# Strassen products whose partial sums add up in PSUM, in a graph-attention layer with a residual and a layer norm

## What is computed

```python
output = einsum('bni,io->bno', x, weight)
q = einsum('bni,io->bno', x, wq)
k = einsum('bni,io->bno', x, wk)
alpha = einsum('bno,bmo->bnm', q, k)
alpha = maximum(alpha, 0.0) * (adj != 0)
alpha = softmax(alpha, axis=1)
y = x + einsum('bnm,bmo->bno', alpha, output)
out = layernorm(y, axis=-1)
```

## Time and profile before

| | |
|---|---|
| Median of 3 timed runs | 557.91 us |
| The profiled execution's own time | 558.32 us |
| Its span, first to last instruction | 556.4 us |
| Mean granted TensorE clock over the span | 0.988 of full |

### The profile page before, as it was taken

How to read it: one execution, slowest core, us unless ns; L and a number is a source line. 1 busy time by engine, 2 the same in 40 slices (tenths; PEclk the granted TensorE clock), 3 DMA queues, 4 the chain that set the end, 5 groups by cost and what they waited for, 6 DMA issues and landing times.

```text
span 556.4 us, 10947 instructions
## 1 busy us (share of the span) xinstructions
PE 530.2 (95%) x3852; PEld 498.4 (90%) x3852; DVE 455.6 (82%) x842; ACT 288.6 (52%) x635; POOL 315.1 (57%) x220
## 2 busy tenths in 40 slices
PE   5886899999999999999999999999999999999994
PEld 4776899899998989999898989989898998989993
DVE  5797769879696988969697896969789796978776
ACT  4744446374553726465373646546364654646263
POOL 2699906639193664919375582928558292844002
PEclk9997999999999999999999999999999999999998
DMA  8206325231432523142152414224150423403021
GB/s 285 93 0 228 114 77 190 75 122 69 140 127 77 188 75 140 48 163 101 75 188 75 158 37 179 79 91 173 75 181 25 171 75 110 154 0 152 0 78 76
DMA packets 23636, 62.12 MB, mean 112 GB/s; under 512 B 1216, under 2 KB 1216, under 8 KB 21696
## 3 DMA queue, kind: packets, MB, share of 16 engines
q1 hardware_dynamic: 23616, 61.87, 30.8%
HBM read 45.09 MB, written 16.78 MB: 111 GB/s over the span
## 4 chain that ended last, share of the span: by engine, by line
PE 67%; DVE 16%; issue 10%; ACT 2%; DMA 2%; SPq 1%; DVEq 1%; POOLq 0%; POOL 0%; ACTq 0%
PE ring L216 13%; PE ring L218 13%; PE ring L217 13%; DVE sums L561 6%; PE s_bank L216 6%; PE s_bank L218 6%; PE s_bank L217 6%; PE o_bank L216 5%; PE o_bank L217 3%; PE o_bank L218 3%; DVE t_lo L547 3%; DMA sums<-in_wk_t 2%; DVE xn L606 2%; ACT t_hi L407 2%; DVE g_lo L547 1%
## 5 line engine op out<-in xcount | busy, mean ns | idle before, releaser
L781 POOL TENSOR_TENSOR s_lo<-xs,s_hi 128x512 fp32r<-128x512 f32 x64 | 92.3, 1455 | 78.8 <-ACT s_hi L396 72.9
L561 DVE TENSOR_TENSOR sums<-sums,ring 128x512 f32<-128x512 f32 x155 | 100.5, 682 | 8.2 <-PE ring L218 7.2
L775 POOL TENSOR_TENSOR a_lo<-xt,a_hi 128x512 fp32r<-128x512 f32 x60 | 94.6, 1605 | 0.0
L432 ACT ACTIVATE squares<-xn,neg_mean 128x512 f32<-128x512 f32 x64 | 46.3, 724 | 86.7 <-DVE neg_mean L613 81.0
L786 POOL TENSOR_TENSOR rstd<-var_eps,minus_half 128x4 f32<-128x4 f32 x15 | 15.3, 1018 | 129.8 <-DVE var_eps L617 129.8
L407 ACT CAST t_hi<-sums 128x512 fp32r<-128x512 f32 x64 | 39.7, 621 | 73.9 <-DVE sums L561 73.1
L216 PE MATMUL s_bank<-t_hi,a_hi 128*128 128x256 f32 x256 | 73.2, 286 | 2.4 <-DVE t_lo L547 2.4
L547 DVE TENSOR_TENSOR v_lo<-sums,v_hi 128x512 fp32r<-128x512 f32 x60 | 72.7, 1228 | 2.3 <-ACT v_hi L412 0.2
L216 PE MATMUL ring<-s_hi,g_hi 128*128 128x256 f32 x256 | 72.7, 284 | 1.4 <-DVE g_lo L547 1.4
L218 PE MATMUL s_bank<-t_hi,a_lo 128*128 128x256 f32 x256 | 73.2, 286 | 0.0
L217 PE MATMUL s_bank<-t_lo,a_hi 128*128 128x256 f32 x256 | 73.1, 286 | 0.0
(11 more groups left out here) (102 smaller groups left out, 1636.0 us busy)
## 6 DMA issues: line engine op xcount, KB each, us to landing
xn<-in_x SPq DMA_DIRECT2D x16, 1024.0 KB, 5.2
xt<-in_x_t SPq DMA_DIRECT2D x15, 1024.0 KB, 4.8
out<-xn SPq DMA_DIRECT2D x15, 1024.0 KB, 4.2
adj<-in_adj_t SPq DMA_DIRECT2D x16, 512.0 KB, 3.3
xt<-in_x_t SPq DMA_DIRECT2D x4, 256.0 KB, 5.2
xn<-in_w SPq DMA_DIRECT2D x4, 256.0 KB, 5.3
xn<-in_wq_t SPq DMA_DIRECT2D x1, 1024.0 KB, 8.7
sums<-in_wk_t SPq DMA_DIRECT2D x1, 1024.0 KB, 10.7
```

The costliest lines, as they stand in the source:

```text
L432: nc.scalar.activation(squares[:], xn[:, slot, r], ACT.Square, bias=neg_mean[:, r:r + 1], accum_out=square_sum[:, r:r + 1]).then_inc(squar ...
L561: nc.vector.tensor_tensor(summed(c), whole, ring[(at + product) % 4][:], op).then_inc(combined, 1)
L775: nc.gpsimd.tensor_tensor(a_lo[:, slot, a], xt[:, a], a_hi[:, slot, a].bitcast(F32), ALU.subtract).then_inc(a_lo_ready, 1)
L781: nc.gpsimd.tensor_tensor(s_lo[:, s], xs[:, s], s_hi[:, s].bitcast(F32), ALU.subtract).then_inc(s_lo_ready, 1)
```

## The change

In T and V the products are now made in 14 half products, each one 128-row half of the result (six matmuls), in a new order: P2,0; P1,0; P1,1; P7,0; P6,0; P6,1; P7,1; P5,0; P5,1; P2,1; P3,0; P3,1; P4,0; P4,1. P1, P6, P5 and P3 accumulate in one place: `chain`, two banks of which T has one half of the columns (`chain_t`) and V the other (`chain_v`). P7 and then P4 accumulate in `bank_y`, and P2 fills `bank_z`. ScalarE copies the chain away after P1 (to c1), after P6 (to c2) and after P5 (to c3), each by halves, six copies, and TensorE waits for the copy of a half before it adds the next product to it. What stands in the chain after P3 is block C12 itself (called A12 as a block of T or V), and is split straight from PSUM. VectorE makes three sums: C22 = c3 + bank_y before P4 is added, C11 = c1 + bank_z, C21 = c2 + bank_y at the end; for the last, the fourth right operand has its sign turned (D4 for T4). They are called A22, A11 and A21 in the splits. T's P1 of the next pair waits until V's part of the chain is split (`v_lo_ready` at `4 * p - 1`). The scaled softmax weights of a pair (`split_p`) move on ScalarE and on VectorE from the V stage of its step into the T stage of the next one, and for pair 15 behind all steps. ScalarE makes a_hi of the next pair behind t_hi of A12, where it was at the head of T.

T of pair 0 is a plain product like V of pair 0: 48 matmuls of 512 columns. It comes ahead of the last quarter of V of pair 0 (now in an `o_bank`). ScalarE writes g_hi straight from PSUM; the G sums T1 to D4 and their splits are only needed by pair 1 but stand on VectorE ahead of the splits of T of pair 0. The sums of x's blocks for pair 0 (GpSimd), with their splits, are gone.

```diff
+        chain = ctx.enter_context(nc.psum_tensor("chain", [P, 2, 2, N], F32))
+        bank_y, bank_z = bank("bank_y"), bank("bank_z")
+        chain_t, chain_v = chain[:, :, 0], chain[:, :, 1]
+        ring = [chain[:, 0], chain[:, 1], bank_y[:], bank_z[:]]
         s_bank = [bank(f"s_bank{i}") for i in range(2)]
         o_bank = [bank(f"o_bank{i}") for i in range(2)]
...
-            def wait_for_bank(i, m):
...
+            def fill_t(p, slot, first=False):
+                m = t_matrix(p)
+                if first:
+                    pe.wait_ge(gt_lo_ready, 4)
                 else:
-                    before = {P1: -PRODUCTS + C22, P6: -PRODUCTS + C12, P5: -PRODUCTS + C11,
-                              P7: -PRODUCTS + C21, P2: U2, P4: U4}[i]
-                    pe.wait_ge(combined, PRODUCTS * m + before + 1)
...
+                    sum_taken(m - 1, 2)
+                x_split(p, 3)
+                t_half(P2, 0, slot, bank_z)
+                if not first:
+                    pe.wait_ge(v_lo_ready, 4 * p - 1)
+                t_half(P1, 0, slot, chain_t)
+                t_half(P1, 1, slot, chain_t)
+                if not first:
+                    sum_taken(m - 1, 3)
+                xs_split(p, 1)
+                t_half(P7, 0, slot, bank_y)
+                copy_taken(m, 1)
+                xs_split(p, 2)
+                t_half(P6, 0, slot, chain_t)
+                copy_taken(m, 2)
+                t_half(P6, 1, slot, chain_t)
+                t_half(P7, 1, slot, bank_y)
...
+                t_half(P3, 0, slot, chain_t)
+                copy_taken(m, 6)
+                t_half(P3, 1, slot, chain_t)
+                sum_taken(m, 1)
+                x_split(p, 4)
+                t_half(P4, 0, slot, bank_y)
+                t_half(P4, 1, slot, bank_y)
...
+            def fill_first_t():
+                for k in range(K):
+                    pe.wait_ge(g_lo_ready, (2, 4, 5, 6)[k])
+                    h, kk = k // 2, k % 2
+                    for j in range(K):
+                        if k == 0 and j < R - 1:
+                            pe.wait_ge(v_lo_ready, j + 1)
+                        last = add_chunk(ring[j], g_parts(k, j), (a_hi[:, 0, h::2, kk], a_lo[:, 0, h::2, kk]),
+                                         k == 0, k == K - 1)
+                        if k == K - 1:
+                            last.then_inc(t0_filled, 1)
...
+            def step(p, slot, first=False):
+                fill_t(p, slot, first)
                 fill_o(p - 1, first)
                 fill_s(p, slot)
-                fill_v(p, slot, at + PRODUCTS, first)
+                fill_v(p, slot, first)
             fill_first_v()
             fill_g()
+            fill_first_t()
             fill_last_of_first_v()
-            fill_first_t()
             fill_s(0, 0, first=True)
-            step(1, 1, PRODUCTS, first=True)
-            step(2, 0, 3 * PRODUCTS)
+            step(1, 1, first=True)
+            step(2, 0)
...
+            def copy_part(m, i, c, src, dst, reader, first=False):
+                if not first:
+                    act.wait_ge(summed, SUMS * (m - 1) + reader)
+                act.wait_ge(filled, HALVES * m + DONE[i, c])
+                nc.scalar.copy(dst[:, c], src[:, c]).then_inc(copied, 1)
+            def copy_p1(m, src, first=False):
+                copy_part(m, P1, 0, src, c1, 2, first)
+                copy_part(m, P1, 1, src, c1, 2, first)
...
+            def split_v(p, u):
+                m = v_matrix(p)
+                if u == A12:
+                    act.wait_ge(filled, HALVES * m + DONE[P3, 1])
+                    whole = chain_v
+                else:
+                    act.wait_ge(summed, SUMS * m + {A22: 1, A11: 2, A21: 3}[u])
+                    whole = {A22: c22, A11: c11, A21: c21}[u]
+                g, j = u // 2, u % 2
+                nc.scalar.copy(v_hi[:, M * g:M * g + M, j], whole).then_inc(v_hi_ready, 1)
...
+            def step(p, slot, more=True, first=False):
+                m = t_matrix(p)
+                copy_p1(m, chain_t, first)
+                split_p(p - 1, 0)
+                copy_p6(m, chain_t, first)
+                split_p(p - 1, 1)
+                copy_p5(m, chain_t, first)
+                split_p(p - 1, 2)
+                act.wait_ge(s_filled, 2 * p)
+                split_t(p, A22)
+                split_p(p - 1, 3)
+                split_t(p, A11)
+                split_t(p, A12)
                 if more:
-                    for k in range(4):
-                        if first and k == 0:
-                            act.wait_ge(v0_filled, R)
-                            act.wait_ge(xt_loaded, 16 * p + 16)
-                            nc.scalar.copy(a_hi[:, 0, A11], xt[:, A11]).then_inc(a_hi_ready, 1)
-                        else:
-                            split_a(p + 1, 1 - slot, k)
-                act.wait_ge(s_filled, 2 * p)
-                for c in SPLITS:
-                    split_t(p, t_matrix(p), c)
+                    split_a(p + 1, 1 - slot, 0)
+                split_t(p, A21)
+                if more:
+                    for k in range(1, 4):
+                        split_a(p + 1, 1 - slot, k)
                 for r in range(R):
                     centred_squares(p - 1, 1 - slot, r)
                 exponent(p, 0)
                 exponent(p, 1)
-                copy_first(v_matrix(p), at + PRODUCTS)
+                m = v_matrix(p)
+                copy_p1(m, chain_v)
                 exponent(p, 2)
+                copy_p6(m, chain_v)
                 exponent(p, 3)
+                copy_p5(m, chain_v)
...
                 if more:
-                    split_s(p + 1, S2, None)
-                for r in range(R):
-                    split_p(p, r)
+                    split_s(p + 1, S3)
+                    split_s(p + 1, S2)
+                act.wait_ge(o_filled, R * p)
+                split_v(p, A22)
                 if more:
-                    split_s(p + 1, S1, None)
-                    split_s(p + 1, S3, None)
-                act.wait_ge(o_filled, R * p)
-                split_v(p, C22)
+                    split_s(p + 1, S1)
+                split_v(p, A11)
+                split_v(p, A12)
                 if more:
-                    split_s(p + 1, S4, None)
-                split_v(p, C12)
-                split_v(p, C11)
-                split_v(p, C21)
+                    split_s(p + 1, S4)
+                split_v(p, A21)
...
+            for j in range(K):
+                split_g(j)
+            for k in range(4):
+                split_a(1, 1, k)
+            for s in S_ORDER:
+                split_s(1, s, first=True)
+            split_gt(T1)
+            split_gt(T2)
+            split_gt(T3)
+            split_gt(D4)
+            for j in range(K):
+                split_first_t(j)
+            for b in W_ORDER:
+                split_wt(b)
             split_first_v(R - 1)
...
-            def combine(m, c, at):
-                product = {U2: P6, U4: P5, U3: P7, C22: P7, C12: P3, C11: P2, C21: P4}[c]
-                dve.wait_ge(filled, PRODUCTS * m + product + 1)
-                before = {U2: None, U4: U2, U3: U2, C22: U4, C12: U4, C11: None, C21: U3}[c]
...
-                nc.vector.tensor_tensor(summed(c), whole, ring[(at + product) % 4][:], op).then_inc(combined, 1)
...
+            def sum_c22(m):
+                dve.wait_ge(copied, COPIES * m + 6)
+                dve.wait_ge(filled, HALVES * m + DONE[P7, 1])
+                nc.vector.tensor_tensor(c22, c3, bank_y[:], ALU.add).then_inc(summed, 1)
+            def sum_c11(m):
+                dve.wait_ge(copied, COPIES * m + 2)
+                dve.wait_ge(filled, HALVES * m + DONE[P2, 1])
+                nc.vector.tensor_tensor(c11, c1, bank_z[:], ALU.add).then_inc(summed, 1)
+            def sum_c21(m):
+                dve.wait_ge(copied, COPIES * m + 4)
+                dve.wait_ge(filled, HALVES * m + DONE[P4, 1])
+                nc.vector.tensor_tensor(c21, c2, bank_y[:], ALU.add).then_inc(summed, 1)
...
-            def step(p, slot, turn, at):
+            def step(p, slot, turn):
                 before = turn if slot == 1 else turn - 1
                 m = t_matrix(p)
-                for c in (U2, U4, U3, C22, C12):
-                    combine(m, c, at)
-                split_t(p, C22)
-                combine(m, C11, at)
-                split_t(p, C12)
-                combine(m, C21, at)
-                split_t(p, C11)
+                split_p(p - 1, 0)
+                split_p(p - 1, 1)
+                sum_c22(m)
+                split_p(p - 1, 2)
+                sum_c11(m)
+                split_t(p, A22)
+                split_p(p - 1, 3)
+                split_t(p, A11)
+                split_t(p, A12)
+                sum_c21(m)
                 residual(p - 1, 1 - slot, before, 0)
-                split_t(p, C21)
+                split_t(p, A21)
...
-                m, at = v_matrix(p), at + PRODUCTS
```

(32 more changed lines are left out.)

469 lines of the change are left out of this document (228 added, 241 removed).

## The result

The changed kernel takes 562.24 us (median of 4 runs, 561.91 to 562.67), the kernel before 558.08 us (4 runs, 556.70 to 558.32): a ratio of 1.0088, 95% interval [1.0068, 1.0108]. So it is slower, as forecast, but by 4.2 us where the sum said 9.9. The profiled execution has a span of 560.2 us against 556.4.

The account below looks back on a forecast made before the run. TensorE, busy 95% of the span, was taken as the bound. Loop 14 x (1.4 - 0.45) = +13.3, start -4.6 and end +1.2 gave +9.9 on 558.3, so 568.2 us; range 549 to 577.

Parts of the forecast that it names:

- The added wait: At the next T's P1, TensorE waits for v_lo of A12: 1.4 us at each of 14 boundaries.
- the two splits stand right behind each other: End of V: VectorE splits A22 and A11 back to back beside GpSimd, the second costing 1.71 us.
- case (b): End of V: both splits cost 1.1, a wait of 0.8, 559.8 us; chance 0.15.
- GpSimd as the cause: End of V: GpSimd's s_lo hold up VectorE's two-SBUF-input splits through an exclusive lock on a shared port.
- O: Output stage, steady loop: TensorE loses 0.37 us a pair against 0.82, so -0.45 us, 14 times.
- a wait of 0.3: In O, the first residual addition is done near 13.0 to 13.1 us after T begins, wanted at 12.81.
- Start: Before the loop: S(0) 0.9 us sooner, step 1 gains 3.6; -4.6 us, bounds -8 and +1.
- End: After the last V: O(15) waits 3.1 us for p_lo, where it waited 1.84; +1.2 us.
- Copies at nothing: Inside a product chain: ScalarE's half copies have some 0.8 us of slack, so TensorE never waits; no cost.
- Rival (c): At every boundary the clock falls behind the gap: +22 us more, 590.6 us; chance 0.08.
- Rival (d): At the start, pair 0's plain product saves nothing; the 4.6 us is lost, 572.8 us; chance 0.07.
- Rival (a): End of V: GpSimd's s_lo miss VectorE's two splits, no boundary wait, kernel faster at 548.6 us; chance 0.25.

Follow-up runs that it names:

- e6: Changed kernel with p_hi and p_lo of all pairs moved back into their own V stage on ScalarE and VectorE: 635.28 us, one run.
- e2: Changed kernel with GpSimd's s_lo covering 8 of 256 columns, the rest zero, TensorE's work unchanged: 545.10 us, one run.
- e1: Changed kernel with block A12 split second, not third, in V, and T's P1 waiting for the second split: 550.76 us, ratio to kernel before 0.9869.
- e8: Changed kernel with T's first residual addition put behind the split of A21 on VectorE: 583.17 us, one run.
- e4: Changed kernel with pair 15's p_hi and p_lo put in its V stage, ahead of the last v splits: 559.71 us, one run.
- e3: Changed kernel with pair 0's T splits ahead of those of the G sums, and t_hi ahead of D4's hi: 559.09 us, ratio to kernel before 1.0026.
- e7b: Changed kernel with A12 split second, pair 0's T splits before G's, pair 2's xt load earlier, pair 15's p in V: 540.28 us, ratio to kernel before 0.9685.
- e5: Changed kernel with T's P1 waiting for the fourth split of V in place of the third: 632.73 us, one run.
- e9b: e7b with T's first residual addition put ahead of the sum C21 on VectorE: 552.58 us, ratio to kernel before 0.9911.

## Why the direction was right and the size was not

- **The added wait: right in place and in cause, mis-sized.** The first failed step is the term "1.4 us at each of 14 boundaries". It measured 1.05, or 1.15 with the first matmul's longer spacing, which the term had left out. The step behind it was that the two splits stand right behind each other, the second at 1.71. They do not: ScalarE's v_hi of A11 comes at 9.7, as the prediction itself had it, and A22's split was done at 9.5. A22's split, at 316.16, finds one s_lo running (it ends by 316.45) and takes 0.85. The next s_lo runs from 316.41 to 318.15. A11's split finds it under way at 317.20, and takes 1.51, where one that stands right behind another takes some 1.7 (e6). That each split pays only for what is left of the s_lo it meets is how I read these rows; no run moved that moment alone. The prediction's case (b), at 1.1 each, was nearer (it gave 0.8).
- **GpSimd as the cause: shown.** e2 takes s_lo away and leaves 0.23 of 1.05. e1 leaves s_lo in place and moves the PSUM split ahead of a split that it blocks; the wait is gone. (ScalarE's v_hi for it comes sooner too in e1, but it wasn't what the split waited for in the kernel after: it was done at 317.65, and the split began at 318.63.) The Trainium skill, SBUF — State Buffer, section "SBUF: two separate sides", says that the shared pair of ports is held for a whole instruction, and that a VectorE operation takes it in a 2-port mode or, against a GpSimd operation that reads SBUF, with two SBUF inputs. The rows agree: 1.51 against 0.69 for parts and v_hi, 0.67 to 0.69 for chain and v_hi in all runs.
- **O: right in direction, half the size.** The second failed step is "a wait of 0.3" for the first residual addition. p_lo cost 0.73, not 1.4, so the addition was done 0.3 ahead of its time and all of the 0.8 came back, against 0.45 forecast. e8 shows how thin that is. The prediction counted this queue from T's beginning as if TensorE did not stop there. But its own wait at P1 holds TensorE and not GpSimd's x sums, and so the splits of T meet less of them. In e1, where the stop is gone, the addition ends at 12.9 after T began, close to the 13.0 to 13.1 forecast, and O loses time again. So the two terms are not independent.
- **The two together** are 14 x (1.15 - 0.73) = +5.9, with 0.73 to 0.82 as the loss of a pair before, against +6.0 in the trace and +13.3 in the sum. Of the 7.4 between them, 14 x (1.4 - 1.15) = 3.5 is the wait and 14 x (0.73 - 0.45) = 3.9 is O. The start and the end came out 1.2 worse than forecast and hid that much of it: 3.8 us of span measured, 9.9 forecast.
- **Start: -3.7 against -4.6.** S(0) starts 0.74 sooner (0.9 forecast) and step 1 gives 3.92 (3.6 forecast), but S(0) takes 8.33 and not the 7.34 that the prediction left unchanged, because the clock is at the lower level for longer behind the 6.98 us gap.
- **End: +1.5 against +1.2**, of which 1.36 is the longer gap. Right, and e4 takes it back.
- **Copies at nothing: right** in the loop. No wait for parts is in the list of the kernel after. One of 1.2 to 1.3 appears in T(1) once the start is earlier (e3, e7b).
- **Rival (c), the clock: wrong at this size, right at three times it.** Behind the gaps of 1.05 it stays at 1.00 over 100 to 500 us; behind those of 3.36 it falls each time (e5).
- **Rival (d)** fell: step 1 takes 31.38, the bare sum. **Rival (a)** did not happen, but e1 shows that it was one swap away (550.8 us, 548.6 forecast for it).

## What to carry to other kernels

When a wait is added for the nth item of a queue, look first at whether that item can be moved up the queue: here one swap was worth 11.5 us, more than the change had cost. Operations with two SBUF inputs on VectorE should be priced by when they begin against GpSimd's running instruction, not by a median or by the worst spacing; keep those that read PSUM for the place where GpSimd is busy. Where a change holds one engine, count again which work of the others then falls beside which: here the added wait moved TensorE against GpSimd, and with it the price of O. And before a step is moved in a queue, ask for each later consumer too what the moved step was covering (e9b), and what the late stage was hiding (e3).
